# Splitting pieces of half the size, twelve row buffers, a shorter index chain and an earlier shared chunk

## The reference, cut to what matters

```
x = x + L0_attn_a(layernorm(x)); x = x + L0_ffn(layernorm(x))
x = x + L0_attn_b(layernorm(x)); x = x + L0_ffn(layernorm(x))      # the same weights again
x = x + L1_attn_a(layernorm(x)); x = x + L1_ffn(layernorm(x))
x = x + L1_attn_b(layernorm(x)); x = x + L1_ffn(layernorm(x))      # the same weights again
# L0_ffn: 8 experts, the two likeliest of each token, and a shared expert behind a gate
shared = (silu(x @ gate) * (x @ up)) @ down * sigmoid(x @ shared_gate_w.T)    # inner width 704
probs, experts = top_k(softmax(x @ gate_w.T), 2)
for e in range(8):
    combined += w_e[:, None] * ((silu(g) * u) @ w2[e].T)       # g, u = x @ w13[e].T, width 176
# L1_ffn: the same with renormalised top-2 weights and an ungated shared expert of inner width 176
```

## Time and profile before

| | us |
|---|---|
| median of 3 runs (1602.2 to 1607.62) | 1602.81 |
| time of the profiled execution | 1605.1 |
| its span, first to last instruction | 1603.0 |
| PE busy | 1475.6 (92%) |
| DVE busy | 990.4 (62%) |
| ACT busy | 756.5 (47%) |
| POOL busy | 534.0 (33%) |

### The profile page before, as it was taken

One profiled execution on the slowest core, in us unless ns is written; L12 is line 12 of the kernel. 1 busy time (PEld: TensorE's weight loads), 2 busy tenths in 40 slices (PEclk: granted clock), 3 DMA queues, 4 the chain that ended last, 5 costly groups with the idle time before them and its releaser, 6 DMA issues. The chain is left out here.

```text
span 1603.0 us, 29414 instructions
## 1 busy us (share of the span) xinstructions
PE 1475.6 (92%) x10844; PEld 1127.3 (70%) x10844; DVE 990.4 (62%) x2156; ACT 756.5 (47%) x1872; POOL 534.0 (33%) x448
## 2 busy tenths in 40 slices
PE   6999999998899989999999989998998898999897
PEld 4778877777788677777777758885555686633587
DVE  5766676666564666666565556557664745476754
ACT  5565656655335334343433434433443353577243
POOL 2836537262137163334133012532000371100074
PEclk9999999999999999999999999989999999999999
DMA  4122221221543532202012018234000633000424
GB/s 153 56 75 90 83 82 59 77 71 64 202 181 103 179 96 86 94 13 96 29 61 78 1 33 340 77 103 173 2 2 5 217 103 115 1 1 1 182 93 138
DMA packets 53900, 144.88 MB, mean 90 GB/s; under 512 B 8721, under 2 KB 23441, under 8 KB 53649
## 3 DMA queue, kind: packets, MB, share of 16 engines
q1 hardware_dynamic: 36496, 84.99, 15.2%
q0 software_dynamic: 17280, 58.21, 10.6%
HBM read 104.90 MB, written 38.27 MB: 89 GB/s over the span
## 5 line engine op out<-in xcount | busy, mean ns | idle before, releaser
L145 POOL TENSOR_SCALAR ln_var<-ln_moments 128x4 f32<-128x4 f32 x16 | 4.0, 251 | 415.9 <-DVE ln_moments L130 261.5
L397 POOL DMA_INDIRECT s_xg<-normed_rows,s_from_row x92 | 93.1, 1012 | 107.0 <-DVE s_from_row L802 80.2
L404 POOL DMA_INDIRECT expert_rows<-s_y,s_to_row x92 | 91.1, 990 | 72.6 <-ACT s_y L688 51.6
L1300 ACT ACTIVATE s_scratch<-s_bank,s_neg_max 128x128 f32<-128x128 f32 (+3 forms) x128 | 67.3, 528 | 89.6 <-DVE s_neg_max L1390 89.4
L1390 DVE TENSOR_REDUCE s_neg_max<-s_bank 128x1 f32<-128x128 f32 (+3 forms) x128 | 59.5, 486 | 54.1 <-PE s_bank L1190 53.9
L1188 PE MATMUL s_bank<-s_k,s_q 128*128 128x128 f32 (+3 forms) x256 | 88.6, 441 | 1.5 <-DVE s_v L1385 0.8
L2699 POOL TENSOR_TENSOR s_w_hi<-s_w_raw,zero 128x1024 fp32r<-128x1024 f32 x25 | 55.7, 2229 | 102.7 <-PE s_memory L81 79.7
L894 DVE TENSOR_TENSOR s_h_e<-s_bank,s_silu_e 128x176 f32<-128x176 f32 x92 | 31.4, 341 | 93.3 <-ACT s_silu_e L676 91.1
L2384 ACT ACTIVATE s_exps<-s_bank,s_rms 128x512 f32<-128x512 f32 x128 | 76.7, 696 | 21.4 <-PE s_bank L2264 21.4
L1400 DVE TENSOR_SCALAR s_scratch<-s_scratch,s_row_sum 128x128 f32<-128x128 f32 (+3 forms) x128 | 80.5, 629 | 4.5
L79 PE MATMUL s_bank<-xn_t_hi,s_w_hi 128*128 128x512 f32 x192 | 80.1, 417 | 0.7 <-DVE s_w_lo L2403 0.4
(11 more groups left out here) (421 smaller groups left out, 4864.6 us busy)
## 6 DMA issues: line engine op xcount, KB each, us to landing
s_expert_w_lo<-experts_lo SPq DMA_DIRECT2D x32, 608.0 KB, 13.5
s_expert_w_hi<-experts_hi SPq DMA_DIRECT2D x16, 608.0 KB, 12.3
s_w_raw<-in_wa_o SPq DMA_DIRECT2D x16, 512.0 KB, 3.6
s_yg<-expert_rows SPq DMA_DIRECT2D x32, 256.0 KB, 4.7
s_raw<-in_shared SPq DMA_DIRECT2D x16, 384.0 KB, 5.5
s_e_lo<-in_experts POOLq DMA_DIRECT2D x16, 304.0 KB, 3.1
experts_hi<-s_e_hi POOLq DMA_DIRECT2D x16, 304.0 KB, 2.5
experts_lo<-s_e_lo POOLq DMA_DIRECT2D x16, 304.0 KB, 2.9
```

The source lines that it names most:

```text
L397: pool.indirect_dma_start(out=xg[:, i % XG_RING, :], out_offset=None, in_=x_rows[:, :], in_offset=bass.IndirectOffsetOnAxis(ap=from_row[:, ...
L404: pool.indirect_dma_start(out=y_rows[:, :], out_offset=bass.IndirectOffsetOnAxis(ap=to_row[:, i:i + 1].bitcast(U32), axis=0), in_=y[:, i % ...
L1300: act.activation(probs[:, h % 2, r, 0:(r + 1) * P], score_bank(h, r), ACT.Exp, bias=neg_max[:, 4 * h + r:4 * h + r + 1], accum_out=row_sum ...
```

## The change

- `XG_RING` is 12: rows 8 to 11 of the ring are the first four tiles of the stage's `xn`, whose rows are in DRAM by then. The results' ring stays at 8.
- The index chain: the comparison reads the integer indices directly; a tile is had by one add and multiply with conversion to integer, twice; the block rows of `tile_hit` are made by POOL and the partition rows by ACT, both after `tile_hit_done`, and `list_rows` waits for both; `slot_hit` is made by 16 instructions of 128 columns.
- Ungated stages: the last chunk's up part is made by PE ahead of the tiles, one half before `list_rows` and one after it, in other PSUM banks; its weights are split ahead of the logits; 12 dummy products stay. Its silu, product, hi and lo, the softmax weights and the diagonal (in two halves) are made before or within the tile loop.
- `ExpertSplit` works each piece in two halves of columns, and the wide stage uses pieces of 608 columns (16 instead of 8): four ahead of the first group, two after each key split, two after each value split.
- The first stage's semaphores are taken from the same pool as the others'.

```diff
-XG_RING, Y_RING = 8, 8
+XG_RING, Y_RING = 12, 8
...
+        def rows_in(i):
+            at = i % XG_RING
+            return xg[:, at, :] if at < Y_RING else norm.xn[:, at - Y_RING, :]
...
+            pool.wait_ge(tile_hit_done, 1)
+            pool.tensor_tensor(tile_hit[:, :, 0, :], tile_hit[:, :, 2, :], spread(block_id, TILES), ALU.mult).then_inc(shares_done, 1)
             pool.wait_ge(x_stored, 16 * NHALF)
             pool.wait_ge(rows_known, 1)
             for i in range(XG_RING):
...
+            def up_last(half):
+                pe.wait_ge(raw_lo_done, n_shared)
+                fill(last_bank[half], SH_GATE, n_shared - 1, half).then_inc(gate_ready, 1)
...
+                pe.wait_ge(shares_done, 2)
                 for h in range(2):
                     pe.wait_ge(slot_hit_done, h + 1)
...
-                keep_busy(pe, res, banks[1][:], 9)
+                up_last(0)
             list_rows()
             if not early:
-                keep_busy(pe, res, banks[1][:], 20)
+                up_last(1)
+                keep_busy(pe, res, banks[3][:], 12)
...
-            up(n_first, 0)
-            up(n_first, 1)
+            if early:
+                up(n_first, 0)
+                up(n_first, 1)
...
+            def mark_lanes():
+                act.wait_ge(tile_hit_done, 1)
+                act.activation(tile_hit[:, :, 1, :], tile_hit[:, :, 2, :], ACT.Copy, scale=partition).then_inc(shares_done, 1)
+            if early:
+                shared_run(range(1))
+                mark_lanes()
+                shared_run(range(1, n_first))
+            else:
+                silu_half(0, 0)
+                silu_half(0, 1)
+                mark_lanes()
+                silu_half(1, 0)
+                silu_half(1, 1)
+                high_half(0, 0)
+                high_half(0, 1)
...
-            then(dve.tensor_copy(at_f[:], at8[:, :, 0:TOP_K]))
...
-            then(dve.tensor_scalar(full[:], rank_bank[:, NT * N_EXP:(NT + 1) * N_EXP], float(P - 1), None,
-                                   ALU.add))
-            then(dve.tensor_scalar(full[:], full[:], 7, None, ALU.logical_shift_right))
-            then(dve.tensor_copy(tiles[:], full[:]))
+            then(dve.tensor_scalar(full[:], rank_bank[:, NT * N_EXP:(NT + 1) * N_EXP], (P - 1) / 2, 1.0 / P,
+                                   ALU.add, ALU.mult))
...
-            then(dve.tensor_copy(in_tile_int[:], position[:]))
-            then(dve.tensor_scalar(in_tile_int[:], in_tile_int[:], 7, None, ALU.logical_shift_right))
-            then(dve.tensor_copy(in_tile[:], in_tile_int[:]))
-            dve.tensor_tensor(tile_hit[:, :, 0, :], tile_hit[:, :, 2, :], spread(block_id, TILES), ALU.mult)
-            then(dve.tensor_scalar(tile_hit[:, :, 1, :], tile_hit[:, :, 2, :], partition, None, ALU.mult))
+            then(dve.tensor_scalar(in_tile[:], position[:], -(P - 1) / 2, 1.0 / P, ALU.add, ALU.mult))
             for h in range(2):
-                dve.tensor_tensor(slot_hit[:, some, :], slot_iota[:].unsqueeze(1).broadcast_to([P, ROWS // 2, P]),
-                                  spread(in_slot[:, some], P), ALU.is_equal).then_inc(slot_hit_done, 1)
+                for j in range(h * ROWS // 2, (h + 1) * ROWS // 2):
+                    last = dve.tensor_scalar(slot_hit[:, j, :], slot_iota[:], in_slot[:, j:j + 1], None, ALU.is_equal)
+                last.then_inc(slot_hit_done, 1)
...
             if not early:
                 h_low(0, 0)
                 h_low(0, 1)
-                low(1)
+                h_of(1, 0)
+                h_of(1, 1)
...
+                if not early and i in (4, 5):
+                    h_low(1, i - 4)
+                if not early and i == 7:
+                    softmax()
+                if not early and i == 8:
+                    choose()
+                if not early and i == 9:
+                    weigh()
+                if not early and i in (11, 12):
+                    diagonal(i - 11)
...
-            expert_split = ExpertSplit(nc, ctx, sem, name, res, t["experts1"], t["experts1_parts"], EXP_COLS)
+            expert_split = ExpertSplit(nc, ctx, sem, name, res, t["experts1"], t["experts1_parts"], E_PART)
...
+                for n in range(4):
+                    expert_split.piece(pool, n, n // 2, n % 2 * E_PART, n == 0)
             for i in range(1, GROUPS):
+                for p in range(3):
+                    split(i, (p,))
+                    if by_run and p < 2:
+                        for n in range(4 * i + 2 * p, 4 * i + 2 * p + 2):
+                            expert_split.piece(pool, n, n // 2, n % 2 * E_PART)
...
+        half = self.columns // 2
+        for h in range(2):
+            some = slice(h * half, (h + 1) * half)
+            pool.tensor_tensor(self.hi[:, some], f32(self.lo[:, some]), self.res.zero[:].broadcast_to([P, half]), ALU.add).then_inc(self.hi_done, 1)
+        for h in range(2):
+            some = slice(h * half, (h + 1) * half)
+            pool.wait_ge(self.hi_done, 2 * n + h + 1)
+            pool.tensor_tensor(self.lo[:, some], f32(self.lo[:, some]), f32(self.hi[:, some]), ALU.subtract).then_inc(self.lo_done, 1)
```

More of the change, by code:

```diff
@@ L635, in _ @@
             high(0)
+            if not early:
+                high(1)
             for half in range(NHALF):
@@ L704, in _ @@
                 y_out(i)
-            shared_run(range(n_first, n_shared))
+                if not early and i in (2, 3):
+                    high_half(1, i - 2)
+            if early:
+                shared_run(range(n_first, n_shared))
         @block.vector
@@ L741, in _ @@
             low(0)
+            if not early:
+                low(1)
             dve.wait_ge(tables_loaded, 16)
@@ new lines, in choose, with weigh @@
+            def choose():
+                for k in range(TOP_K):
+                    last = dve.tensor_tensor(mine[:, k, :, :], hit[:, k, :, :], probs[:], ALU.mult)
+                then(last)
+                then(dve.tensor_reduce(chosen[:].rearrange("p t k -> p k t"), mine[:], AX.X, ALU.add))
+            def weigh():
+                if renormalise:
+                    then(dve.tensor_tensor(row_sum[:], chosen[:, :, 0], chosen[:, :, 1], ALU.add))
+                    then(dve.tensor_scalar(row_sum[:], row_sum[:], 1e-20, None, ALU.add))
+                    then(dve.reciprocal(row_sum[:], row_sum[:]))
+                    then(dve.tensor_tensor(token_w[:], chosen[:], spread(row_sum[:], TOP_K), ALU.mult))
+                else:
+                    then(dve.tensor_copy(token_w[:], chosen[:]))
@@ L886, in _, with diagonal @@
+            def diagonal(half):
+                some = slice(half * TB, (half + 1) * TB)
+                dve.tensor_tensor(weight_diagonal[:, some, :], res.ident[:].unsqueeze(1).broadcast_to([P, TB, P]), spread(token_w[:, some, 1], P),
+                                  ALU.mult).then_inc(diagonal_done, 1)
+            if early:
+                shared_run(range(1, n_first))
+                softmax()
+                choose()
+                weigh()
             if owner_is_gated:
```

112 lines of the change are left out of this document (53 added, 59 removed).

## The result

The changed kernel takes 1579.43 us (median of 4 runs, 1578.35 to 1580.30) where the kernel before took 1603.18 beside it: a ratio of 0.985, interval 0.983 to 0.988. The forecast was 1578.3. The profiled execution's span is 1578.4 us against 1603.0, so 24.6 us went, and the sum had 24.5.

What follows compares the result with a forecast made beforehand. POOL's scatter and gather queue was taken to bound the tile stages, with DVE's index chain ahead of them. 8.5 + 5.4 + 3.6 + 3.0 + 4.0 = 24.5 us off the runs' 1602.8 gave 1578.3 us, range 1568 to 1589.

Steps and rivals of the forecast that it cites:

- the sum: Whole kernel: 8.5 + 5.4 + 3.6 + 3.0 + 4.0 = 24.5 us off the profiled execution's 1605.1 us.
- Gated ring: Tile loops of stages 2 and 4: twelve row buffers instead of eight let PE decide, gaining 3.8 and 4.7, together 8.5 us.
- Rival 1: Stages 2 and 4: POOL decides these loops too, 34 steps at 1.38 us taking 47 us; 1583.3 us, chance 0.12.
- Ungated ring: POOL's queue in stages 6 and 8: twelve buffers recover 2.7 of 3.7 us lost per stage, 5.4 for both.
- Index chain: DVE's steps to the row numbers: rows 1.8 us earlier, bounds -0.1 and 2.4; 3.6 us for stages 6 and 8.
- Rival 2: Index chain: DVE and POOL hold each other, compares take 3.4 us and wait 0.9; 1585.1 us, chance 0.12.
- Gated stages: Stages 2 and 4, ahead of the tiles: earlier rows save at most PE's two waits and 0.2, 1.5 us each, 3.0 together.
- Last chunk at nothing: Stages 6 and 8: moving the last chunk's work ahead of or into the tile loops was counted as no gain or cost.
- cover of 3.19 us: Last chunk's weight split on DVE: its 0.9 us fits into the 3.19 us in which DVE waits for the logits.
- Half pieces: Stage 3: halved expert pieces shrink each PE stall to between 0.1 and 0.9 us; 4.0 us gained, bounds 1 and 7.
- no scaling above 1.2 us beside the pieces: Sign for stage 3: with halved pieces, no DVE scaling beside them takes longer than 1.2 us.
- rival 3: Stage 3: halved pieces make weights late, deciding from 11.4 us per piece; 1619 us at 16 us each, chance 0.02.

## Why the prediction was right, term by term

- **Gated ring, 8.5:** right in place and size (8.8, and 8.1 by taking the ring away). Rival 1 was further off than it looked, since its count had one step too many.
- **Ungated ring, 5.4:** came out at 7.1, and the step that failed is "I count it at nothing" for the moved chunk together with "yet the same work returns inside the loop". The ring gives 2.3 to 2.5 us per stage without the move (61.7 and 61.5 to 59.27) and 1.7 to 2.0 on top of it; the move gives up to 1.5 more, because two long gathers go, which DVE's instructions had held. The work that returns inside the loop, cut into smaller instructions, leaves one gather of 1.2.
- **Index chain, 1.8 us:** measured 0.94. The step "both shorter than the compares beside which they run", charged at 0.3, was the wrong one: the hold is 0.58 and the 16 comparisons cost 0.163 each and not 0.13, so that part came out 0.9 late instead of even. Rival 2 was this mechanism, at about half of its price. The Trainium skill's rule of the shared port pair ("SBUF — State Buffer", section Who interferes with whom) agrees with what was measured, and goes further than the prediction took it: it also names DVE instructions with two SBUF inputs beside a GpSimd instruction that reads SBUF, and the two-input comparison was held too (1.853 against 1.211 us). That "the one that starts first" has the ports is not borne out by the recorded starts, though: in three places a scaling that starts 0.01 to 0.47 us ahead of POOL's instruction is held through it (638.88 against 638.92 with the old pieces, 703.86 against 703.87 in the changed kernel timed again, and 639.04 against 639.50 above, where POOL was issuing a DMA until 639.49).
- **Gated stages, 3.0:** 2.0 measured, from the same short chain.
- **Last chunk at nothing, cover of 3.19 us:** the cover was on DVE. On ACT the split stands ahead of the logits' copy and waits for a load; the prediction priced DVE's part and left ACT's wait out. It cost nothing in the profiled execution of the result (8.5 and 8.5 us against 8.5 and 8.6) and up to 1.5 in others, with another 1.2 to 1.4 on the row numbers where the clock had fallen.
- **Half pieces, 4.0:** right in sum, by errors that cancel. Of the pieces' five stalls (6.8 us) one is left, at 0.50, within "between 0.1 and 0.9"; the rest fell to 0.2 or less or, at 645 us, gave way to another. The sign "no scaling above 1.2 us beside the pieces" came true (at most 1.02), but the pieces are not all that DVE meets. The splits' instructions, which rival 3 lists at 1.89 + 2.5 us, were counted as a delay of the queue and not as a hold of DVE. The longer queue did not make PE wait for weights, as that rival feared, but it brought the value split to the scalings. That cost 4.7 us in this execution. Clock at the start of the stage gave 1.7 and a wait that is not the pieces' 1.0, and neither was forecast.
- **The sum:** the chain's 1.7 + 1.0 us too much stand against 1.7 too little in the ungated queue and 0.3 + 0.3 + 0.5 in the gated loops, the wide stage and the rest. That the total came within 0.1 us is luck. Two stages whose code is the same moved by +1.7 and -1.9 us, and the changed kernel timed once more was 19.4 us faster than the kernel beside it, not 23.8. For the first of the two stages the clock shows why (before, then after, from the start of stage 5); the end of stage 4, just ahead of it, went the other way, 1.65 us shorter at 1.00 where ten us of it ran at 0.79:

```profile
1083.00:1100.00 17.00, 15.02 (x92) 10.27 (x90) 13.36 (x30) 7.97 (x12) 6.90 (x10) 1.00 0.78 290
1100.00:1120.00 20.00, 16.18 (x159) 10.74 (x157) 15.87 (x24) 6.05 (x9) 1.40 (x1) 1.00 0.24 99
```
```profile
1068.00:1085.00 17.00, 16.25 (x100) 12.14 (x98) 14.54 (x30) 7.33 (x12) 8.32 (x10) 0.90 0.93 348
1085.00:1105.00 20.00, 15.95 (x143) 9.54 (x142) 14.19 (x22) 6.11 (x9) 0.00 (x0) 0.91 0.12 50
```

## What to carry to other kernels

When you shorten one engine's instructions because they hold another engine, list every instruction of that engine that can meet the same place; the longest of these sets the next stall, and a new order of the queue can bring it there. Length alone is no price: POOL's move of the queries (3.6 us) holds a scaling for 3.1 us in each later group of both kernels, and no wait of PE follows. A queue of fixed steps is priced by its count times its spacing, and that part of a forecast holds; work moved onto a second engine beside a chain must be charged for the hold as well as for its own time. A step moved ahead of a critical copy needs its data by then: look up when its load lands, not only whether its engine is free.

## What was not expected of the hardware

- A wait of PE is paid twice when its clock falls behind it: 3.50 us of waiting, then 1.2 us more for the next 12 products, at 0.83 of full clock over the ten us (0.50, the lower level, from 645 to 648 us). In the execution without the moved chunk, where the value split came a little later against the scalings, it held one of them (2.49 us), the wait was 1.87 us, and the clock did not fall.
- POOL got in twice in a row between DVE's instructions: each of two neighbouring scalings was held for one whole POOL instruction (2.53 and 2.37 us beside 1.90 and 2.34). Cut in four, POOL's eight instructions took 5.2 us instead of 4.2 and held no scaling there beyond 0.75.
- Gathers that POOL starts beside a DVE instruction of 768 or 1024 columns took 1.72 to 1.91 us instead of 0.95, in each of the four ungated stages profiled with these instructions there. Moving the instructions took the long gathers away, and the ends say the same: all 26 gathers of over 1.6 us in the fourteen profiles, the gated stages' among them, start 0.03 to 0.16 us after such an instruction starts and end 0.815 to 0.826 us after it ends.
